# Paced indirect transfers and a wider down projection in a routed expert layer

## The reference, cut to what matters

```
def _L0_ffn_ref(x, w_gate, W1, b1, W2, b2):
    flat_x = x.reshape(-1, D)                       # 4096 tokens x 128
    gate = jax.nn.softmax(flat_x @ w_gate.T, axis=-1)
    topk_scores, topk_idx = jax.lax.top_k(gate, TOP_K)          # 2 of 8
    cw = (jax.nn.one_hot(topk_idx, N_EXPERTS) * topk_scores[..., None]).sum(axis=1)
    h = jax.nn.gelu(jnp.einsum('td,edh->teh', flat_x, W1) + b1, approximate=False)
    y = jnp.einsum('teh,ehd->ted', h, W2) + b2      # 512 hidden -> 128, the down projection
    out = jnp.einsum('ted,te->td', y, cw)
...
x = x + 0.5 * _L0_ffn_ref(_layernorm(x), ...)       # first application
x = x + _L0_attn_ref(_layernorm(x), ...)            # state-space layer
x = x + 0.5 * _L0_ffn_ref(_layernorm(x), ...)       # second application
```

## Time and profile before

| | us |
|---|---|
| median of 3 executions | 2890.67 |
| range of the 3 | 2889.35 to 2893.76 |
| the profiled execution | 2894.75 |
| its span in the trace | 2893.0 |
| first experts phase, about | 125 to 419 |
| second experts phase, about | 662 to 956 |
| TensorE busy, share of the span | 75% |
| VectorE, ScalarE, GpSimd busy | 61%, 47%, 31% |
| mean TensorE clock granted, share of full speed | 0.88 |

### The profile page before, as it was taken

One profiled execution on the slowest core, in us unless ns is written; L12 is line 12 of the kernel. 1 busy time (PEld: TensorE's weight loads), 2 busy tenths in 40 slices (PEclk: granted clock), 3 DMA queues, 4 the chain that ended last, 5 costly groups with the idle time before them and its releaser, 6 DMA issues. The chain is left out here.

```text
span 2893.0 us, 57024 instructions
## 1 busy us (share of the span) xinstructions
PE 2167.6 (75%) x18046; PEld 1597.7 (55%) x18175; DVE 1756.1 (61%) x3286; ACT 1367.6 (47%) x2902; POOL 908.3 (31%) x700
## 2 busy tenths in 40 slices
PE   4378683654959348888778888886788878888878
PEld 2268571233949226666446666443566654666654
DVE  4445363653626438887358887444788834788844
ACT  2134231121424036666456665566566646566646
POOL 3421213044040414444124444110444411544411
PEclk8589695866979669999889999889899979999979
DMA  9411111001111211011001101000101000110101
GB/s 350 156 49 53 45 46 53 0 30 53 50 51 49 68 45 27 22 26 24 1 9 23 26 22 24 1 3 0 27 22 26 22 8 0 27 26 22 26 4 29
DMA packets 100978, 111.74 MB, mean 39 GB/s; under 512 B 15982, under 2 KB 72088, under 8 KB 100760
## 3 DMA queue, kind: packets, MB, share of 16 engines
q1 hardware_dynamic: 90616, 87.82, 10.8%
q0 software_dynamic: 9408, 20.99, 2.2%
q10 hardware_dynamic: 864, 1.84, 0.2%
HBM read 36.48 MB, written 44.30 MB: 28 GB/s over the span
## 5 line engine op out<-in xcount | busy, mean ns | idle before, releaser
L1567 POOL TENSOR_TENSOR att_sums<-att_turned 128x1024 f32<-128x1024 f32 x128 | 302.6, 2364 | 368.4 <-DVE att_turned L1458 338.0
L1458 DVE TENSOR_TENSOR att_turned<-banks,tables 128x512 f32<-128x512 f32 x512 | 317.5, 683 | 43.6 <-ACT att_squares L1360 43.6
L1574 POOL TENSOR_TENSOR att_qkn<-att_sums,att_rc 128x1024 f32<-128x1024 f32 x128 | 243.7, 1904 | 266.1 <-DVE att_rc L1473 229.4
L1389 ACT ACTIVATE att_probs<-banks,att_nmax 128x128 f32<-128x128 f32 x1024 | 289.0, 375 | 13.4 <-DVE att_nmax L1483 13.4
L1483 DVE TENSOR_REDUCE att_nmax<-banks 128x4 f32<-128x512 f32 x256 | 175.3, 686 | 138.1 <-PE banks L1274 132.4
L54 PE MATMUL banks<-wqkv_h,att_hh 128*128 128x512 f32 x384 | 178.9, 466 | 104.2 <-DVE att_qt L1478 67.0
L1396 ACT ACTIVATE att_pts<-banks 128x512 f32<-128x512 f32 x256 | 140.4, 595 | 139.0 <-PE banks L1283 138.9
L1296 PE MATMUL banks<-att_v_even,att_pts 128*64 128x65 f32 x2048 | 148.2, 227 | 53.2 <-ACT att_pts L1396 31.8
L1382 ACT ACTIVATE att_kt<-banks 128x512 f32<-128x512 f32 x128 | 76.3, 596 | 235.2 <-PE banks L1257 235.2
L1296 PEld LDWEIGHTS banks<-att_v_even,att_pts 128*64 128x64 f32 x2048 | 133.6, 141 | 81.4 <-issue 81.0
L1360 ACT ACTIVATE att_squares<-banks 128x1024 f32<-128x1024 f32 x128 | 131.3, 1026 | 89.2 <-PE banks L56 89.2
(11 more groups left out here) (360 smaller groups left out, 5650.4 us busy)
## 6 DMA issues: line engine op xcount, KB each, us to landing
att_v_even<-att_v SPq DMA_DIRECT2D x224, 130.0 KB, 2.2
y_sorted<-x SPq DMA_DIRECT2D x3, 6528.0 KB
moe0e_xs<-x_sorted SPq DMA_DIRECT2D x88, 64.0 KB
moe1e_xs<-x_sorted SPq DMA_DIRECT2D x88, 64.0 KB
y_sorted<-moe0e_y SPq DMA_DIRECT2D x80, 64.0 KB
y_sorted<-moe1e_y SPq DMA_DIRECT2D x80, 64.0 KB
x_sorted<-blank SPq DMA_DIRECT2D x2, 1088.0 KB, 17.7
raw_w<-in_L_ffn_W POOLq DMA_DIRECT2D x4, 512.0 KB
```

Source lines behind the costliest of these rows:

```text
L1389: act.activation(probs[:, r * HP + p, :], m.ps[:, S + r, p * P:(p + 1) * P], ACT.Exp, bias=nmax[:, r, p:p + 1]).then_inc(exped, 1)
L1458: turn = dve.tensor_tensor(turned[:, i, k, :].rearrange("q (h s j) -> q h s j", s=2, j=DH // 2), q[:, :, ::-1, :] if i else q, table.unsqu ...
L1567: pool.tensor_tensor(sums[:], turned[:, 0, :, :], turned[:, 1, :, :], ALU.add).then_inc(added, 1)
L1574: pool.tensor_tensor(qkn[:, t % 2, :, :].rearrange("q k (h d) -> q k h d", d=DH), sums[:].rearrange("q k (h d) -> q k h d", d=DH), rc[:].u ...
```

## The change

Two edits, in both applications.

**GpSimd waits.** After each second group of tokens, thus after every four indirect transfers, GpSimd waits until all those issued so far have landed. This holds for the 32 transfers of dispatch (L488), and for the 32 writes and the 32 fetches of the experts phase (L692, L700). The fetches of combine (L762) stay as they were.

**The down projection** takes the high and the low weights of a block, which lie side by side, as one moving operand of 256 columns: `gh` times both in one matmul, into columns 0 to 255 of the bank, and `gl` times the high weights in a second one of 128 columns, into columns 0 to 127. That makes 8 matmuls for 12. The low product now stands in columns 128 to 255, so VectorE adds it in a second instruction of 128 columns: the first writes `y` and increments a new semaphore, VectorE waits for that, and the second adds the other half of the bank to `y`.

```
+BURST = 2
...
                         pool.indirect_dma_start(
                             x_sorted[:, :], bass.IndirectOffsetOnAxis(ap=route.index[:, n, k, t:t + 1], axis=0),
                             route.xt[:, n, t, :], None).then_inc(scattered, 16)
-            pool.wait_ge(scattered, 16 * TOP * TT * NH_SEQ)
+                    if t % BURST == BURST - 1:
+                        pool.wait_ge(scattered, 16 * TOP * (TT * n + t + 1))
...
-                bank = m.ps[:, YB[q % 2], :P]
+                bank = m.ps[:, YB[q % 2], :]
                 flat = w.w2[:].rearrange("p e k s d -> p (e k s d)")
                 for k in range(HC):
-                    at = lambda half: flat[:, bass.ds(e * (HC * 2 * P) + (2 * k + half) * P, P)]
-                    pe.matmul(bank, gh[:, q % 2, k, :], at(0), start=k == 0, stop=False)
-                    pe.matmul(bank, gh[:, q % 2, k, :], at(1), start=False, stop=False)
-                    mm = pe.matmul(bank, gl[:, q % 2, k, :], at(0), start=False, stop=k == HC - 1)
+                    at = lambda n: flat[:, bass.ds(e * (HC * 2 * P) + k * 2 * P, n)]
+                    pe.matmul(bank[:, :2 * P], gh[:, q % 2, k, :], at(2 * P), start=k == 0, stop=False)
+                    mm = pe.matmul(bank[:, :P], gl[:, q % 2, k, :], at(P), start=False, stop=k == HC - 1)
                 mm.then_inc(down_done, 1)
...
-                dve.tensor_tensor(y[:, q % GROUP, :], m.ps[:, YB[q % 2], :P], w.b2[:, bass.ds(e * P, P)], ALU.add).then_inc(y_done, 1)
+                dve.tensor_tensor(y[:, q % GROUP, :], m.ps[:, YB[q % 2], :P], w.b2[:, bass.ds(e * P, P)], ALU.add).then_inc(y_copied, 1)
+                dve.wait_ge(y_copied, START + ROUND * i + q + 1)
+                dve.tensor_tensor(y[:, q % GROUP, :], m.ps[:, YB[q % 2], P:2 * P], y[:, q % GROUP, :], ALU.add).then_inc(y_done, 1)
...
 (experts, writes)
                             route.xt[:, n, t, :], None).then_inc(scattered, 16)
+                    if t % BURST == BURST - 1:
+                        pool.wait_ge(scattered, 16 * TOP * (TT * (n - NH_SEQ) + t + 1))
...
 (experts, fetches)
-            pool.wait_ge(gathered, 16 * TOP * TT * NH_SEQ)
+                    if t % BURST == BURST - 1:
+                        pool.wait_ge(gathered, 16 * TOP * (TT * n + t + 1))
```

More of the change, by code:

```diff
@@ L521, in experts_phase @@
         x_turned, xh_done, split, up_done, biased = (sem(n) for n in ("x_turned", "xh_done", "split", "up_done", "biased"))
+        y_copied = sem("y_copied")
         scattered, gathered = c.zero_sem(f"{name}_scattered"), c.zero_sem(f"{name}_gathered")
```

## The result

| us | before | changed |
|---|---|---|
| median of 4 executions | 2890.73 | 2732.84 |
| range | 2889.35 to 2893.76 | 2730.70 to 2733.52 |
| profiled execution, its span | 2894.75, 2893.0 | 2730.70, 2728.8 |

The changed kernel took 0.9451 of the time of the kernel before (95% interval 0.9435 to 0.9468), 5.5% less. 2724 was forecast. On another chip the same two kernels stand at 0.9917 (0.9895 to 0.9939), with 2713.6 us for the kernel before; the experiments come to that.

The account below looks back on a forecast made before the run. TensorE was taken to bound the steady stretches, with late signals during GpSimd's transfers. From the profiled 2894.75 us, -68 (projection), -88 (experts phase) and -11 (dispatch) gave 2727.8, so 2724 at the median; range 2650 to 2845.

Parts of the forecast that it names:

- projection -68: Down projection, both applications: eight matmuls take 0.93 us instead of 1.37, so 0.44 less on each steady tile, 68 us.
- experts phase -88: GpSimd's waits in the experts phase: 71 us lost to stalls, 27 still lost, so 44 gained in each application.
- little to spare: Down projection: VectorE's second addition stays hidden, with 0.43 us of slack left of 0.87 before TensorE needs `gl`.
- rival 4: Down projection: the wide matmul costs like a 512-column one, or VectorE becomes the bound; no gain, 2792 us, chance 0.08.
- What there is to gain, 141: Experts phases: 38.7 us lost under the fetches and 32 under the writes, 141 for both applications.
- What of the stall is left, 1.8 us a burst: Experts phase: each burst of four transfers still loses 1.8 us (30%), between none and all of its 6.04.
- Rival 1: GpSimd's transfers: the stall goes entirely, since four in flight are too few; 2670 us, chance 0.25.
- rival 2: GpSimd's transfers: the waits do nothing for TensorE, since the rate of issue counts; 2855 us, chance 0.15.
- rival 5: Slower: a begun stall lasts until GpSimd is silent 5.2 us, so pauses never end it; +65 us, 2888 in all, chance 0.05.
- Landing, 1.3 us: GpSimd's waits: landing takes 1.3 us behind a burst's last transfer, making a burst of four 6.04 us instead of 5.04.
- Rival 3: GpSimd's waits: landing takes longer than 1.3 us, 2.4 by the first application's row; 2748 us, chance 0.1.
- First dispatch, +2.6: First application's dispatch: four bursts of 10.1 us under the zero fill, four of 6.04; +2.6 us, between +19 and -14.

Follow-up runs that it names:

- down_only: The changed kernel without its waits, one wait put back at each end, so the eight-matmul down projection alone: 2659.5 us, 0.9807 of the kernel before, chip 15.
- before_again: The kernel before, unchanged, run once more for its trace on chip 1, which does not stall: 2713.6 us.
- experts_two: The changed kernel with no waits in dispatch and one after every two transfers in the experts phase: 2656.9 us, 0.9794 of the kernel before, chip 15.
- waits_only: The kernel before plus the changed kernel's waits after every four transfers, down projection still twelve matmuls: 2739.4 us, 1.0103 of the kernel before, chip 15.
- the pauses: The changed kernel with GpSimd clearing a scratch row after every four transfers instead of waiting for landing: 2675.6 us, 0.9859 of the kernel before, chip 15.

## Why the prediction was right, point by point

**Sum.** 2727.8 was worked out for the profiled execution, which took 2730.7. The terms: projection -68, experts phase -88, dispatch -11, in sum -167; measured -155.6 in the experts phases and -11.8 in dispatch, +3.7 behind them. That the sum came so near is in part luck: the projection was put 12 us too high (68 for 56) and the gain from the waits in the experts phase 11 too low (88 for 99), and the two cancel.

**Down projection, -68: mechanism right, size too large.** 0.93 for the eight matmuls was good (0.95), and a 256-column matmul with its 128-column partner takes 0.95 / 4 = 0.24, so half of the 512-column price was a good pick between the bounds. (The 0.46 that stands beside the 0.44 should read 0.48: 1.37 - 4 x 0.109 - 4 x 0.114.) Failed: "in the steady tiles of both applications: 0.44 x 77 x 2". Eight tiles take 18.3 us instead of 21.2, 0.37 a tile: at the turn of the loop TensorE idled about 0.4 before (0.35 to 0.52) and idles 0.8 now. That overhead seems to have lain partly under matmuls that are gone. down_only, against before_again, shows the whole term: 26.8 + 29.1 = 56 us, 0.35 for each of 160 tiles. I had asked what hides VectorE's addition and not what the removed matmuls hid.

**VectorE.** 0.29 and a signal: right, at 0.03 for the signal. TensorE waits for `gl` for 0.8 us in 155 us of experts_two, so the "little to spare" sufficed, and rival 4 is out.

**What there is to gain, 141.** Measured 72.7 + 70.2 = 143. Counting tiles by stretch and pricing the pipeline's start gave the loss to 2 us.

**What of the stall is left, 1.8 us a burst.** 27 us for an application were forecast, 23.4 and 20.8 measured, 1.4 to 1.6 a burst. The pick between "none" and "all" stood on two observations, 5.5 us until the stall begins and 5.2 until it ends. The first is seen again: the lag in the fence above sits at a burst's end. The second is not: after four transfers the lag was over within 2.4 us. So the reason for which I let the stall outlast a pause fails, and the time lost lies within the burst. In dispatch a burst of four delays VectorE's indexes not at all. The 1.8 was a near pick and not a derived one. Rival 1 (all goes) is wrong for fours and nearly right for pairs; rival 2 (the waits do nothing) and rival 5 are out.

**Landing, 1.3 us.** As idle time from the end of the issuing instruction it was mostly 1.5 after writes and 1.8 after fetches, with single bursts at 2.1 to 3.1, so a burst took 6.3 and 6.5 us for 6.04. Rival 3's 2.4 is out but for single bursts. That cost 2 us in the second dispatch (72.5 us, and -12.5 for a forecast of -13.6). Here the Trainium skill, "DMA: Bandwidth & Descriptors", section "Anatomy of one DMA", named about 2.0 us; counted in this way most waits of the trace lie between it and my row.

**First dispatch, +2.6.** Measured +0.7: three bursts under the fill at 10.5 to 11.2, not four at 10.1. That the waits set VectorE free and GpSimd ends the phase was right for both dispatches.

**What the prediction did not see** is where its weight lay. Of the 164 us, 99 are (72.7 + 70.2) - (23.4 + 20.8), a cure for something that five of six later chips did not have, and in dispatch the waits pay for themselves only because they cure another 20.3 + 19.9. On the chips without the stall both gains are zero, the waits of dispatch cost 29 us (21.1 + 8.4, waits_only), and the change is worth 0.8%. Nothing in one trace could tell that. In hindsight one sign was there: a loss that the trace ascribes to nothing ("issue", or a signal long sent) may have a cause outside the program's text, and then it need not be the same elsewhere.

**Still open.** What in a chip, or around it, makes it stall; what is late inside TensorE; and whether landing, silence or a lower rate cures it. How late things are, the fetches of the kernel before show, with a tile's fourth transpose and GpSimd's last fetch:

```profile
300.94 0.37 PE L555 MATMUL banks<-ident,moe0e_g 128*128 128x128 f32 x1 [1.73 <-issue]
...
314.15 0.94 POOL L700 DMA_INDIRECT route_yg<-y_sorted,route_index  x1 [0.30 <-issue]
```

The transpose ends at 301.3, and ScalarE's copy, which waits for nothing but signals of TensorE, starts at 320.63, 19.3 us later. Against landing speaks that even 32 fetches in a row leave no queue behind. The last was issued until 315.1 (not 315.4, as I had worked out), and GpSimd, which waits for all, goes on at 316.7:

```profile
L512 POOLq COMPARE_BRANCH  x2: 38/38/38, 316.7 to 855.1; - x2
```

With 1.3 to 1.8 us to land at 1.25 per transfer, no more than about two should be in flight, waits or no waits. And landing takes some 6 us under the zero fill of the first dispatch and 1.3 in the second, yet both lose the same, 20.3 and 19.9 us. That is argued, not shown: the pauses never ran on a chip that stalls.

## What to carry to other kernels

Before a wait is added to cure a stall that the trace doesn't explain, run the kernel before on several chips: here one cure was worth about 4% on one chip (99 + 12 of 2891 us) and cost 1% on another (waits_only). Put such a wait where the waiting engine has slack (GpSimd in the experts phase: free on the chips without the stall) and not where that engine would become the bound (dispatch: 3 to 37 us). And where instructions are taken from the engine that bounds, look for the fixed overhead that they covered, a loop's turn above all: it took an eighth of the gain here.

## What the runs showed of the hardware that was not expected

- The same kernel, with the same rows for GpSimd's transfers, takes 2707 to 2719 us on chips 1, 2, 4, 9 and 15 and 2889 to 2903 on two measurements elsewhere (one of them chip 13). The difference lies in the phases where GpSimd issues indirect transfers: what waits for TensorE's signal, or TensorE itself, starts late there, in the lines above by 19.3 us.
- On such a chip the loss in an experts phase is 70 to 73 us for 32 in a row twice, 21 to 23 in fours, 1 to 2.5 in pairs. In dispatch it is 20 us for 32 in a row, and nothing is seen of it in fours.
- After a burst of GpSimd the wait for landing took mostly 1.5 to 1.9 us, at times 2.1 to 3.1, and 5.7 to 6.3 us under a zero fill of 20 MB by another queue.
- VectorE waiting for its own previous instruction by a semaphore cost 0.03 us.
